# Residual and running sums on GpSimd instead of VectorE in a conditional-LoRA and feed-forward kernel

## The reference

```
h   = x W^T + bias + (x A[id]^T) B[id]^T        # 2048 x 2048 product and a rank-16 adapter
q   = h Wq^T                                    # 64 wide; router scores, top 8 of 512 slots, softmax
z   = weighted values Wvd^T                     # 128 wide
u   = 0.5 * log1p(var(h)) / mean(log1p(var(h))) + 2.5 * sigmoid(gelu(h Wu1^T + bu1) Wu2^T + bu2)
g   = gate(u), set to 0 below 0.05
out = x + h + g * (z Wvu^T)
```

## Time and profile before

| | |
|---|---|
| median of 3 runs | 2161.21 us (2156.95 to 2161.42) |
| span of the profiled execution | 2157.6 us |
| TensorE matmuls, busy | 2121.8 us (98%), 9510 instructions |
| TensorE weight loads, busy | 1736.1 us (80%) |
| VectorE, busy | 1217.1 us (56%), 1995 instructions |
| ScalarE, busy | 796.0 us (37%), 1193 instructions |
| GpSimd, busy | 2.5 us, 10 instructions |
| DMA | 359.29 MB, mean 167 GB/s |

### The profile page before, as it was taken

How to read it: one execution, slowest core, us unless ns; L and a number is a source line. 1 busy time by engine, 2 the same in 40 slices (tenths; PEclk the granted TensorE clock), 3 DMA queues, 4 the chain that set the end, 5 groups by cost and what they waited for, 6 DMA issues and landing times.

```text
span 2157.6 us, 28213 instructions
## 1 busy us (share of the span) xinstructions
PE 2121.8 (98%) x9510; PEld 1736.1 (80%) x9510; DVE 1217.1 (56%) x1995; ACT 796.0 (37%) x1193; POOL 2.5 (0%) x10
## 2 busy tenths in 40 slices
PE   7999999999999999999999999999999999999998
PEld 5888888888878887888788878888888788888886
DVE  4545655665565556555565565557556644444445
ACT  4433433443343334333433343335334432222221
POOL 0000000000000000000000000000000000000000
PEclk9999999999999999999999999999999999999999
DMA  7554543454444444544454445445444366666668
GB/s 241 169 163 152 187 140 128 158 177 141 130 162 160 134 146 135 182 134 134 149 168 130 146 136 180 135 141 175 152 133 149 112 198 213 214 213 214 216 218 297
DMA packets 160987, 359.29 MB, mean 167 GB/s; under 512 B 21172, under 2 KB 22196, under 8 KB 160758
## 3 DMA queue, kind: packets, MB, share of 16 engines
q1 hardware_dynamic: 105590, 257.16, 38.2%
q10 hardware_dynamic: 55296, 100.69, 12.5%
HBM read 257.11 MB, written 100.66 MB: 166 GB/s over the span
## 4 chain that ended last, share of the span: by engine, by line
PE 94%; DVE 2%; issue 1%; DMA 1%; ACT 1%; SPq 0%; ACTq 0%; DVEq 0%
PE bank L1108 21%; PE bank L1110 21%; PE bank L1109 21%; PE bank L1164 6%; PE bank L1166 5%; PE bank L1165 5%; PE bank L1044 1%; PE bank L1127 1%; PE bank L1045 1%; PE bank L1198 1%; PE bank L1200 1%; PE bank L1199 1%; PE bank L1034 1%; PE bank L1035 1%; PE bank L1086 1%
## 5 line engine op out<-in xcount | busy, mean ns | idle before, releaser
L1108 PE MATMUL bank<-xh,wsp 128*128 128x512 f32 x2048 | 808.9, 395 | 15.7 <-issue 12.6
L1110 PE MATMUL bank<-xh,wsp 128*128 128x512 f32 x2048 | 803.6, 392 | 0.0
L1109 PE MATMUL bank<-xl,wsp 128*128 128x512 f32 x2048 | 803.1, 392 | 0.0
L1108 PEld LDWEIGHTS bank<-xh,wsp 128*128 128x128 f32 x2048 | 387.4, 189 | 100.8 <-issue 14.5
L1110 PEld LDWEIGHTS bank<-xh,wsp 128*128 128x128 f32 x2048 | 387.0, 189 | 82.7
L1109 PEld LDWEIGHTS bank<-xl,wsp 128*128 128x128 f32 x2048 | 387.5, 189 | 80.2
L687 DVE TENSOR_TENSOR wsp<-wraw,wsp 128x1024 fp32r<-128x1024 f32 (+1 forms) x387 | 322.7, 887 | 203.6 <-ACT wsp L425 203.6
L425 ACT ACTIVATE wsp<-wraw 128x1024 fp32r<-128x1024 f32 (+1 forms) x258 | 266.9, 1079 | 375.3 <-PE bank L1045 373.5
L792 DVE TENSOR_TENSOR stage<-stage,xl 128x512 f32<-128x512 f32 x128 | 88.6, 692 | 454.6 <-ACT stage L571 454.6
L571 ACT ACTIVATE stage<-bank,bias_sb 128x512 f32<-128x512 f32 x128 | 88.0, 687 | 548.8 <-PE bank L1127 548.8
L1164 PE MATMUL bank<-h_sp,xh 128*128 128x512 f32 x512 | 204.7, 400 | 2.5 <-DVE h_sp L687 2.5
(11 more groups left out here) (137 smaller groups left out, 1684.1 us busy)
## 6 DMA issues: line engine op xcount, KB each, us to landing
wraw<-in_w SPq DMA_DIRECT2D x129, 544.0 KB, 4.8
wraw<-in_w SPq DMA_DIRECT2D x129, 512.0 KB, 3.6
xraw<-in_x SPq DMA_DIRECT2D x136, 256.0 KB, 4.8
h_dram<-stage ACTq DMA_DIRECT2D x128, 256.0 KB, 2.0
r_dram<-stage ACTq DMA_DIRECT2D x128, 256.0 KB, 2.3
xraw<-h_dram SPq DMA_DIRECT2D x128, 256.0 KB, 2.8
xraw<-r_dram SPq DMA_DIRECT2D x120, 256.0 KB, 3.7
out<-stage ACTq DMA_DIRECT2D x112, 256.0 KB, 3.9
```

What stands on the lines that cost most here:

```text
L1108: pe.matmul(acc_ps, w_hi, xh[:, k, :], start=(k == 0), stop=False)
L1109: pe.matmul(acc_ps, w_hi, xl[:, k, :], start=False, stop=False)
L1110: last_k = pe.matmul(acc_ps, w_lo, xh[:, k, :], start=False, stop=False)
```

## The change

The two adds of the residual and the two running sums go from VectorE's program to GpSimd's, in the same order of tiles, tile 15 of row 7 too. Each sum is still one instruction in a tile. ScalarE also waits for the sum of h of the tile before last before it writes h (VectorE's own order covered that), and stats_pass waits for both sums. VectorE keeps the low half of h and everything else.

```diff
@@ gpsimd
+            def residual(b, o):
+                n = b * KT + o
+                slot = o % 2
+                h_tile = stage[:, slot, :]
+                r_tile = stage[:, 2 + slot, :]
+                wait(pool, h_ready, n + 1)
+                wait(pool, xl_ready, b * KT + o + 1)
+                wait(pool, r_out[slot], 16 * (b * (KT // 2) + o // 2))
+                pool.tensor_tensor(r_tile, h_tile, xl[:, o, :].bitcast(f32), ALU.add).then_inc(rx_ready, 1)
+                wait(pool, rx_ready, n + 1)
+                pool.tensor_tensor(r_tile, r_tile, xh[:, o, :].bitcast(f32), ALU.add).then_inc(r_ready, 1)
+
+            def sums(b, o):
+                n = b * KT + o
+                h_tile = stage[:, o % 2, :]
+                if o == 0:
+                    wait(pool, stats_done, b)
+                    pool.tensor_copy(sum_h[:], h_tile).then_inc(s1_ready, 1)
+                else:
+                    wait(pool, s1_ready, n)
+                    pool.tensor_tensor(sum_h[:], sum_h[:], h_tile, ALU.add).then_inc(s1_ready, 1)
+                wait(pool, sq_ready, n + 1)
+                if o == 0:
+                    pool.tensor_copy(sum_hh[:], sq[:]).then_inc(s2_ready, 1)
+                else:
+                    wait(pool, s2_ready, n)
+                    pool.tensor_tensor(sum_hh[:], sum_hh[:], sq[:], ALU.add).then_inc(s2_ready, 1)
+
+            pool.wait_ge(setup_pe, 2)
+            for o in range(KT):
+                residual(0, o)
+                sums(0, o)
+            for b in range(1, NB):
+                for o in range(KT):
+                    residual(b, o)
+                    sums(b, o)
@@ scalar, row
                     wait(act, hl_ready, n - 1)
+                    wait(act, s1_ready, n - 1)
@@ vector, row
-                    if first and o == 0:
-                        dve.wait_ge(setup_pe, 2)
-                    if not (last and o == KT - 1):
-                        residual(b, o)
...
-                    if o == 0:
-                        wait(dve, stats_done, b)
-                        dve.tensor_copy(sum_h[:], h_tile).then_inc(s1_ready, 1)
-                    else:
-                        wait(dve, h_ready, n + 1)
-                        wait(dve, s1_ready, n)
-                        dve.tensor_tensor(sum_h[:], sum_h[:], h_tile, ALU.add).then_inc(s1_ready, 1)
                     wait(dve, hh_ready, n + 1)
                     lo(h_sp[:, slot, 1, :], h_tile, h_sp[:, slot, 0, :]).then_inc(hl_ready, 1)
...
-                    wait(dve, sq_ready, n + 1)
-                    if o == 0:
-                        dve.tensor_copy(sum_hh[:], sq[:]).then_inc(s2_ready, 1)
-                    else:
-                        wait(dve, s2_ready, n)
-                        dve.tensor_tensor(sum_hh[:], sum_hh[:], sq[:], ALU.add).then_inc(s2_ready, 1)
@@ vector, row2
-                            residual(NB - 1, KT - 1)
@@ tensor, stats_pass
+                wait(pe, s1_ready, (b + 1) * KT)
                 wait(pe, s2_ready, (b + 1) * KT)
```

## The result

The changed kernel takes 2182.55 us (median of 4, 2180.95 to 2183.49) against 2161.32 us (2156.95 to 2161.51): 21.2 us slower, a ratio of 1.0105 with a 95% interval of 1.009 to 1.0119. The direction was forecast (0.51 for slower), the size was not: 2167.8 us was forecast, and the time lies just above the range's end of 2182.0.

What follows compares the result with a forecast made beforehand. TensorE was taken as the bound, busy 2121.8 of 2157.6 us. The middle of -1.4 us (gains alone) and +14.5 us (full hold-up), +6.6 us, added to the median 2161.2 gave 2167.8 us; range 2158 to 2182.

Steps and rivals of the forecast that it cites:

- A GpSimd add takes 1.2 us: Estimate for a two-input add of 512 columns, built from fill and affine_select rows, within bounds of 0.52 and 1.9 us.
- the added waits of ScalarE or stats_pass: New waits for GpSimd's sums before ScalarE writes h and before stats_pass; put at nothing while GpSimd keeps up.
- Rival 2: Every ordinary tile stalls TensorE at L1044, the low half of h being 0.2 us late: 2190 us; chance 0.11.
- the upper bound: Each VectorE or GpSimd instruction waits for the whole of the other's, first come first served: +14.5 us.
- The layout: Row end under full hold-up: xl[15] 3.8 us late, 13.6 us of stalls in sum, +14.5 us in all.
- the middle of -1.4 and +14.5 us: Between no hold-up (gains alone) and full hold-up of VectorE and GpSimd, the forecast took +6.6 us.
- the four jump gaps: TensorE's 12.6 us of waits without a shown cause where the row loop jumps back; forecast as untouched.
- margin against a stall: Time from xl[15]'s end to the last LoRA step at a row end: 1.9 us, 1.6 us for row 6.
- The stalls for xl: Under full hold-up, TensorE stalls 1.9 us at six row ends and 2.2 us after row 6: 13.6 us.
- The 0.5 us to be won at v_sp: TensorE's 0.5 us wait for v_sp after row 0, counted among the gains of removing VectorE's adds.
- The slow stretches behind longer waits: Lower granted clock after TensorE stalls, three times 1.6 us, counted only in the range's upper end.
- The start of phase two: TensorE's wait for a split of h: up to 1.3 us sooner without hold-up, 1.6 us later with full hold-up.

## Why the prediction was wrong in size

- **TensorE is the bound and there is little to win: right.** The most that the freed VectorE gave was 4.3 us, in the run whose GpSimd doesn't read.
- **A GpSimd add takes 1.2 us: right**, 1.30 alone. GpSimd kept up, and none of the added waits of ScalarE or stats_pass cost anything, as the prediction had it.
- **No new wait in ordinary tiles: right.** The low half of h starts sooner and meets one add. Rival 2's stall in most tiles can happen, though: it appeared when the residual stayed on VectorE.
- **The two engines hold each other up in full: the upper bound, and it holds.** The layout had GpSimd and VectorE alternate, a w split wait for the second residual add and the sum go ahead of xl[15]; the row end above shows each of these. The Trainium skill ("SBUF — State Buffer", Who interferes with whom) was right as far as these rows go: reads against reads collide for whole instructions, and GpSimd's fills don't collide.
- **The step that failed: taking the middle of -1.4 and +14.5 us.** These were two mechanisms, not a quantity known within limits, so their middle was a time that neither gives. The run with only writes on GpSimd is the one end, the changed kernel the other. By its own upper layout the prediction would have said 2175.7 us; halving it accounts for 7.9 of the 14.6 us by which +6.6 fell short of 21.2.
- **The second step that failed: "the change doesn't touch them", of the four jump gaps.** They were put at nothing without a reason and grew by 7.1 us, from 12.6 to 19.7: the 2 us of matmuls between xl[15] and the end of the row, which the prediction counted as margin against a stall, also hid a part of the jump. So the margin can cost at these row ends before a wait for xl appears: the gaps were 19.3 us with tile 15 on VectorE and 23.9 us with the sums there, and neither run waits for xl.
- **The terms of that layout.** The stalls for xl were put at 13.6 us and measured 9.2: at this row end xl[15] ended 20.3 us after h of tile 14, against 17.6 us before, so 2.7 us late and not 3.8. The layout had h of tile 15 1.6 us late; it came 14.8 us after h of tile 14 instead of 14.1, so 0.8 us late.
- **What else was left out.** The 0.5 us to be won at v_sp had the wrong sign: v_sp stands behind the late splits on VectorE, and the wait went up by 2.6 us. The slow stretches behind longer waits were in the range only, not in the sum; they are the 3.6 us of longer busy time. The start of phase two, put at 1.6 us worse, kept its sum nearly: 3.1 us of waits at L1052 and L1173 against 0.8 and 2.5 us before.
- **The range.** Its upper end is said to be the full layout and three slow stretches of 1.6 us; that gives 2180.5 us, not the 2182 stated.

## What to carry to other kernels

Work on an idle engine is not free if its reads and those of a busy engine shut each other out, as here. Before work is moved from VectorE to GpSimd, look which two-input VectorE instructions will run beside it, and which of them stand on a chain with little to spare; in the rest of this kernel the collision was harmless. Where two mechanisms are possible, forecast one of them and not the middle. Time to spare ahead of a jump may not be spare: it can be what hides the jump. And a half of a change can be much worse than the whole: what counts is what stands ahead of the urgent instruction in its own queue.

## What the runs showed of the hardware

- A VectorE add, subtract or split with two inputs in SBUF and a GpSimd add, both 128x512 float32, take turns for whole instructions. Alone they take 0.69 and 1.30 us; where they meet, VectorE's is recorded with 1.17 to 1.79 us and GpSimd's with 1.6 to 2.3 us, the wait included.
- A VectorE copy of 512 columns with its one input in SBUF takes turns too: in the run with the sums on VectorE, `sum_hh<-sq` took 0.42 us alone and 1.50 to 1.52 us where it met a GpSimd add.
- VectorE instructions with one input in PSUM kept their 0.69 us beside GpSimd (`wt_sp<-bank,wt_sp` at 630.36 above, while GpSimd's second add ran).
- GpSimd fills beside VectorE cost VectorE nothing (692 ns).
- TensorE's jump back over a loop body of some 1900 matmuls and weight loads left it idle for 2.7 to 6.1 us in these runs. A 16 KB transfer of instructions began in each of these gaps, and the first matmul followed 2.6 to 2.7 us behind it in all but the run with copies ahead of the jump (up to 3.2 us). Written out, the same work was 1% faster.
- The granted clock was 0.57 over the 3.6 us behind a gap of 3.4 us, and 0.50 over the 5.8 us behind one of 5.2 us.
